# Router products by column groups of TensorE, the second attention's state over normalised tokens, and new orders in both passes

## The chip, the cores and the metric

One Trainium2 chip, one core of it. The metric is the device time of one execution in microseconds. The kernel before was timed three times. The core has TensorE (PE: matmuls; PEld: its weight loads), VectorE (DVE), ScalarE (ACT), GpSimd (POOL) and the engine that issues most DMAs (SP). Each works through a program of its own in order, and they meet in semaphores.

## The reference, cut to what matters

Two layers over 8 x 1024 tokens of 256 features, each an attention and a mixture of 8 experts. The change touches the router of both mixtures and the second attention:

```
# router, both layers:  logits = tokens @ gate.T          (256 features -> 8 experts)
#                       top1 = argmax, rank by cumsum, keep while rank < capacity
# second attention, per batch of 1024 tokens, x = layernorm(tokens):
qkv = einsum('bnd,ed->bne', x, W_qkv);  q, k, v = split(qkv, 3)
q = relu(q) + 1e-6;  k = relu(k) + 1e-6
kv = einsum('bnd,bne->bde', k, v)
z = 1 / (einsum('bnd,bd->bn', q, k.sum(axis=1)) + 1e-6)
out = einsum('bnd,bde,bn->bne', q, kv, z) @ W_out.T + b_out
x = x_in + layernorm(out)
```

## The kernel before, in words

The 8192 tokens are 16 groups of 512 (four tiles of 128); two groups, a pair, are one batch. Products that need full precision are made of three fp32r matmuls (high x high, high x low, low x high: `three`), so each operand is kept as a high part (ACT, a copy that rounds) and a low part (DVE, value minus high part).

The program has these stages: a memory part; pass 1 (loop `for s in range(1, 14)`: first attention, gate, feed-forward and router of layer 1, a group per step, each step working on groups s-2 to s+3); the 8 experts of layer 1; pass 2 (loop over pairs: second attention and router of layer 2); the 16 expert halves of layer 2. Expert tokens are scattered to DRAM by POOL's indirect DMAs and read back by SP.

The order in each engine is written out by hand, as one loop per engine with the calls of several groups interleaved. Nothing reorders it. PE's results go through a ring of three PSUM units (`Ring`, two banks each; `unit` takes the next one and waits until the reader of its last content has freed it) beside one accumulator, `acc`. So the call that comes three units later waits for the ACT or DVE instruction that empties a unit.

The router (`logits`, L707 to L714): for each of four tiles and two halves of the features one fp32 matmul with the tile's 128 x 128 tokens as weights and 8 columns of the gate's weights moving; it gives tokens on partitions, and DVE (`route1`) takes the argmax. `route1` leads to the one-hot rows, PE's `prefix` to the ranks, `route2` to the slots, POOL's `scatter` to DRAM.

The second attention. ACT normalises a group into `xnA` (`xl_norm`), PE turns it (`xl_t`), ACT and DVE split it (`xl_high`, `lows`). PE then makes `queries` (12 matmuls of 512 columns), `keys` (24 of 512 columns: K and the values V, already folded with W_out, side by side) and `state` (24 of 256 or 258 columns: K transposed times V, with a column of ones for the sum of the keys). DVE applies relu and 1e-6 (`q_relu`, `k_relu`), ACT copies V (`v_copy`) and rounds (`kv_high`, `q_high`), DVE subtracts (`kv_low`, `q_low`). At a batch's end ACT and DVE split the accumulated state (`kw_high`, `kw_low`), and a pair later PE makes `att_out` (24 of 258 columns per group). `unread` is matmuls whose result nobody reads; they stand where PE would be idle.

## Time and profile before

| | us |
|---|---|
| median of 3 runs | 1897.04 |
| lowest, highest | 1894.91, 1899.98 |
| profiled execution, its span from first to last instruction | 1900.1 |
| PE, PEld busy in it | 1843.4, 1631.5 |
| DVE, ACT, POOL busy | 1496.8, 1069.6, 624.2 |
| pass 2 (1180 to 1477) | 297 |

The profiled execution has only its span; what lies around the first and the last instruction is not in the trace. Busy times are unions of the instructions' durations. A matmul's duration contains its latency, and following matmuls overlap it, so that what one costs PE is read as the distance from start to start.

### The profile page before, as it was taken

The page shows a single profiled execution, that of the slowest core. Times are in us where ns is not written, and L with a number is a line of the kernel's source. Part 1 is how long each engine was busy: PE and PEld are TensorE (multiplying, and loading weights), DVE is VectorE, ACT ScalarE, POOL GpSimd, SP SyncE. Part 2 cuts the span into 40 slices and gives each one's busy share as a digit, 9 for nine tenths or more (in the row PEclk, how much of TensorE's full clock was granted, in tenths as well). Part 3 has the DMA queues.
Part 4 walks back from the last instruction along what each step waited for, and adds up shares of the span by engine and source line. Part 5 has one row for each costly group of instructions (what it writes and reads, how often), then busy time and mean ns, then how long its engine had stood idle before and what let it go on. Part 6 is the DMA issues. An engine that isn't in the chain of part 4 may idle for free.

```text
span 1900.1 us, 31592 instructions
## 1 busy us (share of the span) xinstructions
PE 1843.4 (97%) x11542; PEld 1631.5 (86%) x11542; DVE 1496.8 (79%) x3901; ACT 1069.6 (56%) x1734; POOL 624.2 (33%) x927
## 2 busy tenths in 40 slices
PE   8999999999999999999899999999999999999996
PEld 7888878888888888888779998888988799999996
DVE  7777579999999999999748884789998566666663
ACT  5656725566566665666456663665564255555552
POOL 3211001234433333444604443134534312333333
PEclk9999999999999999999899999999999899999998
DMA  5545242222222221201143422134322312222210
GB/s 178 163 150 167 81 153 68 90 86 95 89 84 83 94 82 64 78 26 37 51 152 124 134 87 89 60 119 135 100 89 76 90 60 82 93 83 86 76 51 18
DMA packets 132610, 176.95 MB, mean 93 GB/s; under 512 B 11486, under 2 KB 115813, under 8 KB 132328
## 3 DMA queue, kind: packets, MB, share of 16 engines
q1 hardware_dynamic: 121704, 159.87, 26.3%
q0 software_dynamic: 10752, 15.06, 2.3%
q8 instruction: 92, 1.51, 0.3%
q14 instruction: 62, 0.51, 0.1%
HBM read 113.25 MB, written 76.51 MB: 100 GB/s over the span
## 4 chain that ended last, share of the span: by engine, by line
PE 86%; DVE 5%; ACT 2%; POOL 2%; DMA 2%; issue 2%; SPq 0%; POOLq 0%; DVEq 0%; ACTq 0%
PE ps L385 78%; PE ps L409 4%; PE ps L712 2%; PE ps L701 1%; POOL d_p L2587 1%; DVE bst L1614 1%; PE ps L470 1%; DMA stage<-in_w 0%; DMA stage<-in_wi 0%; DVE rO L2155 0%; DMA xa<-in_x 0%; DVE wslotA L1820 0%; DMA d_x<-df 0%; DVE pay L1939 0%; DVE kl L1639 0%
## 5 line engine op out<-in xcount | busy, mean ns | idle before, releaser
L385 PE MATMUL ps<-wslotA,fh 128*128 128x256 f32 x1776 | 326.1, 284 | 0.0
L1830 DVE TENSOR_TENSOR fl<-fF,fh 128x512 fp32r<-128x512 f32 x316 | 214.0, 683 | 94.2 <-ACT fF L1209 93.3
L385 PEld LDWEIGHTS ps<-wslotA,fh 128*128 128x128 f32 x1776 | 280.4, 191 | 5.2 <-DVE fl L1830 0.2
L385 PE MATMUL ps<-wslotA,fl 128*128 128x256 f32 x888 | 251.2, 283 | 0.0
L2582 POOL TENSOR_TENSOR smalls<-smalls,powers 128x4 f32<-128x4 f32 x87 | 28.0, 321 | 591.7 <-DVE smalls L1617 591.6
L2587 POOL DMA_INDIRECT d_p<-pay,sut x128 | 154.3, 1205 | 103.7 <-DVE pay L1987 57.4
L385 PE MATMUL ps<-x2h,wslotA 128*128 128x512 f32 x512 | 171.0, 396 | 0.2 <-DVE x2l L1639 0.2
L385 PEld LDWEIGHTS ps<-wslotA,fl 128*128 128x128 f32 x888 | 170.0, 191 | 0.0
L1208 ACT ACTIVATE fh<-ps,b1e 128x512 fp32r<-128x512 f32 x126 | 86.9, 690 | 143.0 <-PE ps L385 140.6
L385 PE MATMUL ps<-wslotB,fh 128*128 128x256 f32 x752 | 137.1, 283 | 0.4 <-DVE fl L1830 0.4
L385 PE MATMUL ps<-eh,wslotB 128*128 128x512 f32 x384 | 125.3, 393 | 2.4 <-DVE el L2011 2.4
L385 PE MATMUL ps<-eh,wslotA 128*128 128x512 f32 x384 | 125.5, 393 | 0.7 <-DVE el L1639 0.7
L385 PEld LDWEIGHTS ps<-wslotB,fh 128*128 128x128 f32 x752 | 119.2, 192 | 3.1 <-issue 0.6
L1208 ACT ACTIVATE fh<-ps,cols 128x512 fp32r<-128x512 f32 x128 | 88.6, 692 | 56.6 <-PE ps L385 52.8
L385 PEld LDWEIGHTS ps<-x2h,wslotA 128*128 128x128 f32 x512 | 96.3, 188 | 24.7 <-issue 5.6
L385 PE MATMUL ps<-wslotB,fl 128*128 128x256 f32 x376 | 106.4, 283 | 0.0
L385 PE MATMUL ps<-x2l,wslotA 128*128 128x512 f32 x256 | 100.2, 391 | 0.0
L2587 POOL DMA_INDIRECT out_x<-eq,sut x60 | 69.5, 1159 | 91.1 <-DVE eq L2052 76.9
L2583 POOL TENSOR_TENSOR smalls<-smalls,powers 128x4 f32<-128x4 f32 x87 | 95.4, 1096 | 6.8
L1628 DVE SCALAR_TENSOR_TENSOR xl<-xl,smalls,rows 128x256 f32<-128x256 f32 x192 | 80.0, 479 | 15.6 <-POOL smalls L2583 15.6
L1614 DVE BATCH_NORM_STATS2 bst<-xl 128x6 f32<-128x256 f32 x256 | 89.4, 411 | 0.3
L1209 ACT ACTIVATE fF<-ps,cols 128x512 f32<-128x512 f32 x128 | 88.3, 690 | 0.0
(383 smaller groups left out, 5146.5 us busy)
## 6 DMA issues: line engine op xcount, KB each, us to landing
stage<-in_w SPq DMA_DIRECT2D x16, 1024.0 KB, 5.6
d_p<-blank SPq DMA_DIRECT2D x24, 528.0 KB, 4.8
pay<-d_p SPq DMA_DIRECT2D x24, 528.0 KB, 3.7
d_x<-df SPq DMA_DIRECT2D x16, 516.0 KB, 3.5
xA<-d_x SPq DMA_DIRECT2D x16, 516.0 KB, 3.7
xa<-in_x SPq DMA_DIRECT2D x16, 512.0 KB, 4.9
d_h<-hh SPq DMA_DIRECT2D x16, 512.0 KB, 5.4
d_h<-hl SPq DMA_DIRECT2D x16, 512.0 KB, 3.0
```

The source lines that it names most:

```text
L385: return pe.matmul(o, a, b, start=start, stop=stop, skip_group_check=True)
L409: t = pe.transpose(ps[:, c * 512 + i * 128:c * 512 + i * 128 + 128], x[:, i * stride + c * 128:i * stride + (c + 1) * 128], ident)
L470: t = pe.transpose(ps[:, i * 256 + c * 128:i * 256 + c * 128 + 128], x[:, c * 512 + i * 128:c * 512 + i * 128 + 128], ident)
L712: t = pe.matmul(ps[:, i * 8:i * 8 + 8], x[:, c * 512 + i * 128:c * 512 + i * 128 + 128], w8[:, c, :], start=c == 0, stop=c == 1)
L1208: act.activation(dh[:, half(k)], u.ap[:, half(k)], func, bias=b)
L1209: t = act.activation(df_[:, half(k)], u.ap[:, half(k)], func, bias=b)
L1614: marks.append(mark(ve.bn_stats(b[:, i, :], x[:, i, :])))
L1628: marks = [mark(ve.scalar_tensor_tensor(x[:, i, :], x[:, i, :], m[:, i:i + 1], gain, ALU.subtract, ALU.mult)) for i in range(4)]
L1830: ve.tensor_tensor(dl[:, half(k)], df_[:, half(k)], f32(dh[:, half(k)]), ALU.subtract).then_inc(S["low"], 1)
L2582: last(po.tensor_tensor(t[:, 8:12], mv_of(t)[:, :, 1], eps, ALU.add))
L2583: po.tensor_tensor(t[:, 12:16], t[:, 8:12], mhalf, ALU.pow).then_inc(signal, 1)
L2587: po.indirect_dma_start(dst, bass.IndirectOffsetOnAxis(idx[:, i:i + 1], 0), src[:, i, :], None, bounds_check=bound, oob_is_err=False).then ...
```

## The change

Four things. First, the router's product turns round: the gate's 8 columns are the weights, 128 tokens move, and the four tiles' results go to PSUM partitions 0, 32, 64 and 96, which are four groups of 32 columns of PE's array. ACT then copies the 128 x 128 block to `lgt` (`logits_copy`) and PE turns it back in one transpose (`by_token`), so that `route1` reads tokens on partitions as before.

Second, the state is summed over the normalised tokens U instead of over the values: K transposed times U (256 columns), and once per batch that state times the folded value weights (`state_values`, 12 matmuls of 258 columns). So `keys` makes only K (24 matmuls of 256 columns), and V is never formed. `state_high`, `state_low` split the state, `u_high`, `u_low` the tokens.

Third, since a normalised token's features sum to zero, its last feature is replaced by 1 and the last row of the weights is subtracted from the others (`weights_differences`, once, on DVE in the last expert of layer 1). The column of ones gives the sum of the keys, and 1e-6 sits in a weight row, so that relu(k) + 1e-6 is one maximum: ACT applies Relu as it reads PSUM (`q_high`, `k_high`), DVE takes max and subtracts in one instruction (`q_low`, `k_low`). `q_relu`, `k_relu` and `v_copy` go.

Fourth, the loops of all engines in pass 2 are written anew, the router's calls in pass 1 are moved, the second expert weight block of layer 2 is loaded three pairs later and split in the loop's step 6 instead of step 2, and `unread` calls at the end of pass 2 go, except the last of 52.

PE in pass 1, one step, before, then changed (xl is a group's tokens, x1h and x1l the gate's operand, x2h the feed-forward's, sc the attention's weights, tT the turned tokens):

```order
L385 MATMUL ps<-small,x1h 128x256 x2
L385 MATMUL ps<-small,x1l 128x256
L712 MATMUL ps<-gwT,tT 128x8 x8
L385 MATMUL ps<-xl_93,sc_97 128x258 x2
L385 MATMUL ps<-halo,sc_97 16x258
```

```order
L390 MATMUL ps<-x2l,wslotA 128x512
L390 MATMUL ps<-x2h,wslotA 128x512
L390 MATMUL ps<-tT,gwT 8x128 x8
L390 MATMUL ps<-small,hh_70 128x512 x2
L390 MATMUL ps<-small,hl_72 128x512
```

The eight products have moved ahead of the gate's matmuls; the transpose (L723) stands some 50 rows later, behind the first `w2`:

```order
L390 MATMUL ps<-wslotA,fh_111 128x256 x2
L390 MATMUL ps<-wslotA,fl_113 128x256
L723 MATMUL ps<-ident,lgt 128x128
L390 MATMUL ps<-x2h,wslotA 128x512
L390 MATMUL ps<-x2l,wslotA 128x512
```

DVE in pass 2, a stretch that begins at a group's statistics in a pair's step. Before (kvF is relu(K) beside V, kvl its low part, qF relu(Q), ql its low part, rO the attention's output, pay the tokens for the router, cdt and lgx router rows):

```order
L2135 TENSOR_TENSOR kvl_132<-kvF_130,kvh_134 128x1024
L2126 TENSOR_SCALAR kvF_131<-ps 128x2x256
L1939 TENSOR_TENSOR pay_55<-rO_136,xb_138 128x4x256
L2166 SCALAR_TENSOR_TENSOR smalls<-smalls 128x4
L1614 BN_STATS bst<-pay_55 128x6 x4
L1617 BN_AGGR pay_55<-bst 128x2 x4
L2119 TENSOR_SCALAR qF<-ps 128x1024
L2135 TENSOR_TENSOR kvl_133<-kvF_131,kvh_135 128x1024
L2131 TENSOR_TENSOR ql_144<-qF,qh_141 128x1024
L2126 TENSOR_SCALAR kvF_130<-ps 128x2x256
```

Changed (kk_l is K's low part, ul the tokens', xAl the turned tokens'):

```order
L1997 TENSOR_TENSOR pay_56<-rO_136,xb_138 128x4x256
L2178 SCALAR_TENSOR_TENSOR ql_145<-ps,qh_142 128x1024
L2183 SCALAR_TENSOR_TENSOR kk_l<-ps,kk_h 128x512
L2188 TENSOR_TENSOR ul_133<-xnA,uh_131 128x1024
L2235 SCALAR_TENSOR_TENSOR smalls<-smalls 128x4
L2183 SCALAR_TENSOR_TENSOR kk_l<-ps,kk_h 128x512
L1672 BN_STATS bst<-pay_56 128x6 x4
L1675 BN_AGGR pay_56<-bst 128x2 x4
L1697 TENSOR_TENSOR xAl_127<-ps,xAh_125 128x512 x2
```

Two instructions per half group (kvF from PSUM, kvl over 1024 columns) have become one over 512 columns that reads PSUM, and that one now comes behind ACT's Relu, no longer ahead of ACT.

ACT in pass 2, where tokens are rounded, changed:

```order
L1101 ACTIVATE lgt<-ps 128x128
L1101 ACTIVATE uh_131<-xnA 128x1024
```

The first of the two empties the router's unit; the second waits for the state of the group before last (`u_high` below), and everything of ACT's step behind it waits with it.

The diff, cut to its core:

```diff
             def logits(which, g, x, w8):
-                ps = unit("LG", which, g)
-                for i in range(4):
-                    for c in range(2):
-                        t = pe.matmul(ps[:, i * 8:i * 8 + 8], x[:, c * 512 + i * 128:c * 512 + i * 128 + 128], w8[:, c, :],
-                                      start=c == 0, stop=c == 1)
-                t.then_inc(S["lg"], 1)
+                ps = unit("LA", which, g)
+                for c in range(2):
+                    for i in range(4):
+                        t = mm(ps[32 * i:32 * i + 8, 0:128], w8[:, c, :], x[:, c * 512 + i * 128:c * 512 + i * 128 + 128],
+                               c == 0, c == 1)
+                t.then_inc(S["la"], 1)
+            def by_token(which, g):
+                evacuated("LA", which, g)
+                pe.transpose(unit("LG", which, g)[:, 0:128], lgt, ident).then_inc(S["lg"], 1)
...
             def keys(g, k):
-                    t = three(ps[:, half(i % 2)], [(xAh[g % 2][:, q[c]], xAl[g % 2][:, q[c]], wq_h[:, c, 256:768],
-                                                    wq_l[:, c, 256:768]) for c in range(2)], True, True)
+                    t = three(ps[:, i % 2 * 256:i % 2 * 256 + 256],
+                              [(xAh[g % 2][:, q[c]], xAl[g % 2][:, q[c]], wq_h[:, c, 256:512], wq_l[:, c, 256:512])
+                               for c in range(2)], i % 2 == 0, True)
...
             def state(g, k):
-                        mm(o, hv[:, i, q], hv[:, i, 256:514], first, False)
-                        mm(o[:, 0:256], hv[:, i, q], lv[:, i, 256:512], False, False)
-                        t = mm(o, lv[:, i, q], hv[:, i, 256:514], False, end)
+                        t = three(acc[:, half(c, 256)], [(uh[g % 2][:, q], ul[g % 2][:, q], hv[:, i, :], lv[:, i, :])],
+                                  first, end)
+            def state_values(bt):
+                pe.wait_ge(S["stl"], bt + 1)
+                ps = unit("KW", bt)
+                for m in range(2):
+                    q = slice(m * 128, m * 128 + 128)
+                    t = three(ps[:, half(m, 258)], [(st_h_[:, c, q], st_l_[:, c, q], wx_h[:, c, :], wx_l[:, c, :])
+                                                    for c in range(2)], True, True)
...
+            def logits_copy(which, g):
+                copy(lgt, u.ap[:, 0:128]).then_inc(u.free, 1)
+            def u_high(g):
+                if g >= 2:
+                    act.wait_ge(S["sta"], 2 * (g - 1))
+                act.wait_ge(S["xn_l"], 2 * g + 1)
+                copy(uh[g % 2], xnA).then_inc(S["xn_l"], 1)
             def q_high(g):
-                act.wait_ge(u.free, u.before + 1)
-                copy(qh[g % 3], qF).then_inc(S["qh"], 1)
+                act.wait_ge(S["q"], g + 1)
+                act.activation(qh[g % 3], ring.of("Q", g).ap, ACT.Relu).then_inc(S["qh"], 1)
-            def v_copy(g, k):
-            def kv_high(g, k):
+            def k_high(g, k):
+                act.activation(kk_h[:, half(k)], ring.of("K", g, k).ap[:, 0:512], ACT.Relu).then_inc(S["ksh"], 1)
...
-            def q_relu(g):
-            def k_relu(g, k):
             def q_low(g):
-                ve.tensor_tensor(ql[g % 3], qF, f32(qh[g % 3]), ALU.subtract).then_inc(S["ql"], 1)
+                ve.scalar_tensor_tensor(ql[g % 3], u.ap, 1e-6, f32(qh[g % 3]), ALU.max, ALU.subtract).then_inc(u.free, 1)
+            def k_low(g, k):
+                ve.scalar_tensor_tensor(kk_l[:, half(k)], u.ap[:, 0:512], 1e-6, f32(kk_h[:, half(k)]), ALU.max,
+                                        ALU.subtract).then_inc(u.free, 1)
+            def u_low(g):
+                ve.tensor_tensor(ul[g % 2], xnA, f32(uh[g % 2]), ALU.subtract).then_inc(S["ul"], 1)
+            def weights_differences():
+                last(ve.tensor_tensor(wqk_v, wqk_v, wlast.unsqueeze(1).to_broadcast([128, 2, 512]), ALU.subtract))
...
@@ PE, pass 2 @@
                 if s in PAIRS:
                     queries(2 * s)
+                if s - 1 in PAIRS:
+                    state_values(s - 1)
+                if s in PAIRS:
+                    keys(2 * s, 0)
+                    keys(2 * s, 1)
...
@@ SP @@
-                if s in (0, 1):
-                    weights(19 + s)
+                if s in (0, 4):
+                    weights(19 + s // 4)
```

## Rows read from the trace of the kernel before

**Rows 1.** The page: the span, the engines' busy time, the chain that ended last.
```profile
span 1900.1 us, 31592 instructions
PE 1843.4 (97%) x11542; PEld 1631.5 (86%) x11542; DVE 1496.8 (79%) x3901; ACT 1069.6 (56%) x1734; POOL 624.2 (33%) x927
...
PE 86%; DVE 5%; ACT 2%; POOL 2%; DMA 2%; issue 2%; SPq 0%; POOLq 0%; DVEq 0%; ACTq 0%
```

**Rows 2.** Busy time by stretch; granted clock, DMA share and GB/s last.
```profile
290.00:915.00 625.00, 624.61 (x4088) 550.90 (x4087) 576.93 (x1578) 388.79 (x610) 220.13 (x376) 1.00 0.22 72
...
1180.00:1477.00 297.00, 286.52 (x1871) 256.77 (x1872) 255.11 (x728) 164.68 (x268) 115.78 (x180) 0.98 0.31 95
```

**Rows 3.** The same view, single steps: pass 2, then pass 1.
```profile
1226.31:1262.34 36.03, 31.44 (x188) 28.17 (x187) 30.19 (x74) 23.25 (x36) 11.41 (x20) 0.91 0.42 129
1262.34:1298.13 35.79, 35.79 (x244) 32.15 (x244) 31.82 (x98) 20.96 (x35) 15.68 (x26) 1.00 0.39 115
1298.13:1333.98 35.85, 35.85 (x244) 32.19 (x244) 33.02 (x100) 20.97 (x35) 15.80 (x26) 1.00 0.39 116
410.92:453.55 42.63, 42.63 (x282) 37.42 (x282) 39.62 (x112) 26.84 (x43) 14.88 (x27) 1.00 0.30 101
```

**Rows 4.** PE in order of time, pass 1: start, duration, instruction, count.
```profile
451.85 1.85 PE L712 MATMUL ps<-gwT,tT 128*128 128x8 f32 x16
453.55 3.70 PE L385 MATMUL ps<-xl,sc 128*128 128x258 f32 x14
457.18 0.50 PE L385 MATMUL ps<-x2h,wslotA 128*128 128x512 f32 x1
```

**Rows 5.** PE in order of time, 239 to 242 us.
```profile
239.13 2.08 PE L385 MATMUL ps<-xT 128*128 128x144 f32 x16
241.04 0.52 PE L385 MATMUL ps<-xT,xT 128*128 128x16 f32 x4
241.49 0.60 PE L385 MATMUL ps<-ident,cols 128*1 128x128 f32 x4
242.02 0.33 PE L547 MATMUL ps<-ident,gs 128*128 128x128 f32 x1
```

**Rows 6.** PE in order of time, pass 2.
```profile
1308.87 0.40 PE L385 MATMUL ps<-small,xAl 128*128 128x512 f32 x1
1309.11 0.28 PE L385 MATMUL ps<-kvh 128*128 128x258 f32 x1
...
1310.55 0.40 PE L385 MATMUL ps<-xAh,small 128*128 128x512 f32 x1
...
1313.35 1.04 PE L701 MATMUL ps<-ident,pay 128*128 128x128 f32 x8
```

**Rows 7.** DVE by line and shape, three pairs (1262.34 to 1369.73).
```profile
L2135 DVE TENSOR_TENSOR kvl<-kvF,kvh 128x1024 fp32r<-128x1024 f32 x12 | 14.6, 1215 | 0.0
L2126 DVE TENSOR_SCALAR kvF<-ps 128x512 f32<-128x512 f32 x12 | 8.2, 687 | 3.3 <-PE ps L385 3.1
L1639 DVE TENSOR_TENSOR xAl<-ps,xAh 128x512 fp32r<-128x512 f32 x12 | 7.6, 675 | 0.0
L2119 DVE TENSOR_SCALAR qF<-ps 128x1024 f32<-128x1024 f32 x6 | 7.3, 1225 | 2.7 <-PE ps L385 2.7
L2145 DVE TENSOR_TENSOR small<-ps,small 128x516 fp32r<-128x516 f32 x3 | 2.0, 663 | 0.0
```

**Rows 8.** ACT by line and shape, the same three pairs.
```profile
L1071 ACT ACTIVATE kvh<-kvF 128x1024 fp32r<-128x1024 f32 x12 | 12.8, 1069 | 0.3
L1075 ACT ACTIVATE xnA<-xA,smalls 128x256 f32<-128x256 f32 x24 | 12.4, 588 | 0.0
L1071 ACT ACTIVATE kvF<-ps 128x512 f32<-128x512 f32 x12 | 7.1, 593 | 24.1 <-DVE kvF L2126 24.1
L1279 ACT ACTIVATE lgx<-lgx 128x32 f32<-128x32 f32 x6 | 1.4, 228 | 0.0
```

**Rows 9.** The chain that ended last, in order of time, 1241 to 1256 us.
```profile
1241.92 8.66 DMA stage<-in_w
...
1250.61 1.07 ACT wslotA L1071
...
1255.64 5.50 PE ps L385 x24
```

**Rows 10.** PE in order of time, the end of pass 2 and the first expert.
```profile
1465.77 0.50 PE L385 MATMUL ps<-small,qh 128*128 128x258 f32 x2 [1.89 <-DVE small L2145]
...
1474.03 1.85 PE L712 MATMUL ps<-wgT,tTO 128*128 128x8 f32 x16
...
1511.20 0.50 PE L385 MATMUL ps<-eh,wslotA 128*128 128x512 f32 x1 [0.73 <-DVE el L1639]
```

More of the change, by code:

```diff
@@ L265, in build @@
         xAl = [tile("xAl0", 4, R), tile("xAl1", 8, R)]
-        qF = tile("qF", 6)
-        kvF = [tile("kvF0", 7), tile("kvF1", 18)]
-        kvl = [tile("kvl0", 9, R), tile("kvl1", 10, R)]
-        kvh = [at(f"kvh{i}", TILES_AT + 11 * PAGE + i * 4 * 1032, 1028, R) for i in range(2)]
+        kk_h, kk_l = tile("kk_h", 6, R), tile("kk_l", 7, R)
+        uh = [tile("uh0", 9, R), tile("uh1", 11, R)]
+        ul = [tile("ul0", 10, R), tile("ul1", 12, R)]
+        stt = tile("stt", 13, R)
+        st_h_, st_l_ = v3(stt[:, 0:512], 2, 256), v3(stt[:, 512:1024], 2, 256)
+        wqk_v, wlast = v3(stage[:, 0:1024], 2, 512), stage[:, 1024:1536]
         wv_v = v3(stage[:, 1536:2048], 2, 256)
@@ L950, in tensor_program @@
             logits(0, 15, tT, gwT)
+            unread(a12_h, 2)
+            by_token(0, 15)
             unread(a12_h, 4)
@@ L1020, in tensor_program @@
                     state(2 * s + 1, 1)
-                if s + 1 in PAIRS:
-                    xl_t(2 * s + 3)
+                if s - 1 in PAIRS:
+                    by_token(1, 2 * s - 2)
+            state_values(7)
+            t_t(1, 13)
             prefix(1, 12)
@@ L1329, in values_folded @@
             def values_folded():
                 act.wait_ge(S["vw"], 1)
-                copy(wq_h[:, :, 512:768], two(ring.of("VW").ap)).then_inc(S["vwh"], 1)
+                copy(wx_h[:, 0, 256:258], blank[:, 0:2])
+                copy(wx_h[:, 1, 256:258], ident[:, 127:128].to_broadcast([128, 2]))
+                copy(wx_h[:, :, 0:256], two(ring.of("VW").ap)).then_inc(S["vwh"], 1)
                 act.wait_ge(S["w1"], 8 * (G + E))
-                for k in range(2):
-                    for i in range(2):
-                        copy(v3(kvh[k], 2, 514)[:, i, 512:514], ones[:, 0:2])
+                for i in range(4):
+                    copy(xv(xnA)[:, i, 255:256], ones[:, 0:1])
@@ L1337, in kw_high, with state_high @@
+            def state_high(bt):
+                if bt:
+                    act.wait_ge(S["vw"], bt + 1)
+                act.wait_ge(S["sta"], 4 * (bt + 1))
+                copy(st_h_, v3(acc, 2, 512)[:, :, 0:256]).then_inc(S["kwh"], 1)
             def kw_high(bt):
@@ L2111, in expert_end, with x_low, q_low @@
                     o.then_inc(S["eres"] if h else S["eres_h"], 1)
[L2114 removed]
+            def x_low(g):
+                lows(xAl[g % 2], xAh[g % 2], ring.of("XLT", g), S["xlh"], g)
+            def q_low(g):
                 u = ring.of("Q", g)
[L2116 to L2127 removed]
@@ L2508, in vector_program @@
                     new_x(1, 2 * s - 1)
+                if s in PAIRS:
+                    state_low(s)
+                if s - 1 in PAIRS:
                     route1(1, 2 * s - 2)
+                if s + 1 in PAIRS:
+                    q_low(2 * s + 2)
+                if s - 1 in PAIRS:
                     stats_5th(1, 2 * s - 1)
@@ L2513, in vector_program @@
                 if s + 1 in PAIRS:
-                    lows(xAl[(2 * s + 3) % 2], xAh[(2 * s + 3) % 2], ring.of("XLT", 2 * s + 3), S["xlh"], 2 * s + 3)
+                    k_low(2 * s + 2, 0)
+                    k_low(2 * s + 2, 1)
+                    u_low(2 * s + 3)
+                if s - 1 in PAIRS:
+                    route2(1, 2 * s - 2)
+                if s in PAIRS:
+                    att_out(2 * s, 0)
+                    att_out(2 * s, 1)
+                if s + 1 in PAIRS:
+                    x_low(2 * s + 3)
+                if s in PAIRS:
+                    stats_o(2 * s)
+                    att_out(2 * s + 1, 0)
+                    att_out(2 * s + 1, 1)
+                    nmean_o(2 * s)
+                    stats_o(2 * s + 1)
+                if s - 1 in PAIRS:
+                    route1(1, 2 * s - 1)
+                if s in PAIRS:
+                    new_x(1, 2 * s)
+                if s + 1 in PAIRS:
+                    q_low(2 * s + 3)
+                    k_low(2 * s + 3, 0)
+                if s == 2:
+                    weights_low(19, 0)
+                    weights_low(19, 1)
+                if s == 6:
+                    weights_low(20, 0)
+                    weights_low(20, 1)
             for n in range(E - 1, 3 * E):
@@ L2956, in sync_program @@
             weights(4)
-            load(b1e[:, :], io["eb1_c"], S["b1e"])
+            load(b1e[:, :], io["eb1_c"], S["late"])
             square(wout_v, "WoutT", S["wout"])
```

363 lines of the change are left out of this document (177 added, 186 removed), and 2 rows, old and new, of the table S.

## The prediction

> **What bounds the kernel now.** I read the page first. PE is busy for 1843.4 of 1900.1 us and holds 86% of the chain that ended last [rows 1], so a change pays by what it takes off PE, as long as no other engine steps in. Then the stages: in the main part of pass 1 PE is busy for 624.6 of 625 us at full clock, in pass 2 for 286.5 of 297 [rows 2]. Then single steps: a pair of groups in pass 2 takes 35.8 us, a step of pass 1 about 42.6, with PE busy throughout and DVE busy for 32 to 33 and 39.6 of it [rows 3]. DVE is at 91% and 93%: it is the next bound, and close. Last the distances between PE's starts: twelve matmuls of 512 columns in 1313.35 - 1310.55 = 2.80 us, 0.233 each; twelve of 256 or 258 in 1310.55 - 1309.11 = 1.44, 0.12 each [rows 6].
>
> **Pass 2 on PE, per pair.** `keys` stays at 48 matmuls, of 256 columns instead of 512: 48 x (0.233 - 0.12) = 5.4 us less. `state` keeps its 48 of about 256 columns. `state_values` adds 12 x 0.12 = 1.4. Queries, `att_out` and transposes are unchanged. With the router (next part, 0.25 less per group) the pair comes to 35.8 - 5.4 + 1.4 - 0.5 = 31.3 us.
>
> **The router's products.** Before, a group has 16 records (two per fp32 matmul) in 453.55 - 451.85 = 1.70 us [rows 4]. Afterwards there are 16 again, with 8 weight columns and 128 moving. The nearest row is a product with one weight column and 128 moving ones: four records in 242.02 - 241.49 = 0.53, 0.13 each [rows 5]. To this comes a change of the weights' width. Sixteen fp32 records of 144 columns take 1.91 us [rows 5], 0.83 ns per column, so fourteen of 258 should take 3.0; where widths of 128 and 16 columns alternate they take 457.18 - 453.55 = 3.63 [rows 4] with four changes of width, 0.16 us per change. The new block has two changes, 0.3 us. The transpose back adds about 0.13 (eight took 0.87 or so between neighbours).
>
> If the four column groups really run side by side, the block is four records deep: 4 x 0.13 + 0.3 + 0.13 = 1.0 us, 0.7 less than now. If nothing overlaps, it is 16 x 0.107 to 0.13, plus 0.43: 2.1 to 2.5, that is 0.4 to 0.8 more. No row shows two column groups at once. I take the middle: PE takes matmuls in order and the two records of one product follow each other in the same group, so a product can overlap its neighbour but not itself, which leaves eight of 0.13, 1.0 + 0.43 = 1.45 us, 0.25 less per group. In pass 1, which is PE's alone, that is 16 x 0.25 = 4 us.
>
> The rows show 0.16 us lost at each change of width [rows 4]. The Trainium skill says in TensorEngine Tiling (Array Packing), Tiling Modes, that a change of tiling mode drains the engine; by that rule the 0.3 us stays even where the products overlap in full, and the trace agrees in size.
>
> **Pass 2 on DVE, per pair.** Out go 4 `kvl`, 4 `kvF` and 2 `qF`: (14.6 + 8.2 + 7.3) / 3 = 10.0 us [rows 7]. In come 4 `k_low` over 512 columns out of PSUM, like xAl at 0.68: 2.7; 2 `u_low` over 1024, like kvl, 1.2 each: 2.4; one `state_low`, like the split state, 0.66 [rows 7]: 5.8 together. 32.4 - 10.0 + 5.8 = 28.2 us busy. Before, DVE's 32.4 busy went with a step of 35.8, 90.5%, the rest being gaps between dependent small instructions and waits of a few tenths. At the same share 28.2 gives 31.2 us: DVE reaches PE's 31.3. Neither alone sets the pair any more, and two orders that just touch don't mesh without loss: `q_low` and `k_low` now come behind ACT's Relu (1.07 for 1024 columns, 0.59 for 512 [rows 8]) where DVE used to read PSUM first. The PSUM unit is thus held for ACT plus DVE (about 1.3 us for K, 2.3 for Q), and three units later PE wants it. I take 31.7 per pair; bounds 30.5 (PE with the router overlapped in full) and 34. Eight pairs: 8 x (35.8 - 31.7) = 33 us less.
>
> ACT: out go 4 `kvh` (4.3 us) and 4 `kvF` copies (2.4); in come 4 K roundings (2.4), 2 `u_high` (2.1), `state_high` (0.6) and two copies of 128 columns (between the 0.23 of 32 columns and 0.59 [rows 8], 0.6 together). 21 busy becomes 20 of 31.7 [rows 3, 8]: it does not bound by its sum, only by its place (rival E).
>
> **The second weight block.** In the step 1226 to 1262 PE is busy for 31.4 of 36.0 us, at clock 0.91 [rows 3]: the block's load lands at 1250.6, ACT and DVE then split it, and PE starts again at 1255.6 [rows 9]. The load now comes three pairs earlier than its split, so this 4.6 us wait goes. What is late next in that step is DVE with 30.2 busy, so I count 3 less (0 to 5).
>
> **What gets longer.** At the last batch's end PE now waits for split state, product and split product instead of one split. Before, one split kept PE waiting for 1.89 us [rows 10]; the second one (0.6 ACT, 0.66 DVE) and the product (1.44) are partly covered by a transpose and `prefix`: +2. In the other batches `queries` (2.8 us) covers the first split, and two K blocks with a transpose (3.7) the second; if DVE runs late, this is where it shows. `weights_differences` puts a 1024-column subtraction (1.2) and smaller ones on DVE ahead of `low(2, 0)` in the last expert of layer 1: +1. From the last `att_out` (1474.0) to the first expert of layer 2 (1511.2) there are 37 us [rows 10] that DVE, ACT, POOL and DMAs set; the `unread` calls removed there only filled PE's idle time. The router's extra step costs one ACT copy and one transpose (0.5 us with hand-over) and gives back what PE's block loses: 0. The same at the end of pass 1. In pass 1 the transpose comes only after the first `w2`, and `route1` some 6 us later than before; `prefix` is 20 us away and the feed-forward's low parts have about 4 us in hand before PE asks for them, so nothing is late.
>
> **The sum** against the profiled execution: 1900.1 - 33 - 3 - 4 + 2 + 1 = 1863. The timed median lies 3.1 us below that span (1897.0 against 1900.1), so I predict 1860 us.
>
> **The rivals.**
> A. The forecast: 1860, own range 1850 to 1870. Chance 0.5.
> B. The column groups overlap in full: 0.45 us less per group than in A, 7 us in pass 1; in pass 2 PE's pair is 30.4 and DVE sets it at 31.2, another 4 or 5. For it: consecutive products go to different groups. Against: the two records of one product do not. Time 1848. Chance 0.2. The Trainium skill, TensorE: Matmul & The Clock Gate, Part 3 (Packing small matmuls), gives 4 ns per further tile and a measured 2.38 times for three column tiles: by its model this is the case, while its in-order rule is what A rests on. No run here shows either yet.
> C. They don't overlap, and PE only gets two changes of width and a transpose: 2.1 to 2.5 us per block. Against A that is 0.65 to 1.05 x 16 = 10 to 17 us; in pass 2 half of it is hidden behind DVE, so 8 to 13 in all for pass 1 and 4 to 8 more. 1881. Chance 0.13.
> D. DVE takes over in pass 2: the products gain as in A, but gaps bring the pair to 34 us, 8 x 2.3 = 18 more: 1878. For it: 28.2 busy within 31.7 leaves as little as before, with more hand-overs per step. Against: DVE's share before was the same and cost PE 0.0 idle in two steps [rows 3]. Chance 0.1.
> E. Slower than before: the single buffer `xnA`. A group's tokens are normalised (4 x 0.59 [rows 8]), turned, rounded by `u_high`, subtracted by `u_low`, and only then may the next be normalised; `u_high` also waits for the state of the group before last, and ACT's queue stands behind it: the output's normalisation, Q's and K's Relu, hence PSUM units, hence PE. I find ACT free some 3 us before that state ends in each pair's middle. If each group's block of 3.2 us reached PE, 16 x 3.2 = 51 more: 1911. It decides from (1897 - 1860) / 16 = 2.3 us lost per group. Against: DVE has work queued in that time, and only one of a pair's two groups is placed so tightly. Chance 0.07.
>
> **From these the range.** B's and C's ends give 1842 to 1882; outside lie E and a slice of C and D. Less than 0.3% (5.7 us) is no change that a measurement of this kernel can tell. A to D are faster by more, 0.93 less a little for a mixture of C, D and E that just cancels: 0.91 faster, 0.03 the same, 0.06 slower.
>
> **What the changed profile would show.** The router's 16 records start over about 1.3 us (A), 0.8 (B) or 1.7 to 2.1 (C), and a pass 1 step is 42.3, 41.9 or 43 us. A pair in pass 2 takes about 31.7 with PE above 97% busy; at 34 or more with waits of PE on DVE low parts it is D, with waits on `xnA` and ACT idle before `uh` it is E. No idle of 4.6 us before a `base` or `kvl` instruction. Wrong would be the whole sum if the pair stayed above 34, or if the 37 us between passes grew with PE's clock down for want of the `unread` calls.

## The result and the profile after

| | kernel before | changed kernel | ratio, 95% interval |
|---|---|---|---|
| median | 1897.63 us (1894.91 to 1899.98, 4 runs) | 1887.68 us (1886.32 to 1889.31, 4 runs) | 0.9948 [0.9936, 0.9960] |
| span of the profiled execution | 1900.1 us | 1884.6 us | |

The change makes the kernel 0.5% faster. Forecast were 1860 us and a range of 1842 to 1882: the sign was right, the size was not. The medians differ by 10.0 us and the profiled spans by 15.5. Where both are known, the timed value lies 1.7 us above the span (1886.32 and 1884.6 for the profile of the changed kernel); the profiled execution of the kernel before was thus a slow one (about 1901.8, an estimate, above all four timed ones), and that of the changed kernel the fastest of its four. Of the balance below, 5.5 us are this. First the page of the changed kernel: the head, busy times by engine, and the chain that ended last.

```profile
span 1884.6 us, 31885 instructions
PE 1787.1 (95%) x11647; PEld 1576.6 (84%) x11647; DVE 1467.6 (78%) x3884; ACT 1067.6 (57%) x1760; POOL 632.8 (34%) x927
PE 70%; DVE 14%; POOL 6%; issue 5%; ACT 3%; DMA 2%; SPq 0%; another core or an unknown queue 0%; POOLq 0%; DVEq 0%; ACTq 0%
```

PE has lost 56 us of busy time (1843.4 before [rows 1]), but the span fell by 15.5 only, and PE's share of the chain fell from 86% to 70%. DVE and POOL took it. Where, the busy times by stretch say (columns: stretch, length, then busy us of PE, PEld, DVE, ACT and POOL with counts, granted clock, DMA share, GB/s): pass 1, one of its steps, pass 2, and the end of pass 2.

```profile
293.00:890.00 597.00, 575.79 (x3782) 498.74 (x3781) 536.95 (x1474) 360.33 (x566) 206.44 (x347) 0.98 0.22 72
524.00:568.50 44.50, 41.56 (x280) 36.05 (x280) 40.81 (x114) 27.26 (x43) 17.45 (x31) 1.00 0.27 90
1200.00:1458.00 258.00, 240.52 (x1975) 221.40 (x1975) 218.47 (x690) 155.37 (x271) 118.42 (x179) 1.00 0.35 110
1458.00:1505.00 47.00, 33.43 (x186) 26.68 (x186) 25.23 (x98) 14.46 (x27) 17.32 (x22) 0.75 0.29 90
```

In pass 1, where PE was busy for 624.6 of 625 us [rows 2], it now idles 21 of 597. A step took 42.6 us [rows 3]; it now takes 44.5 (43.9 and 45.1 by turns; the first two, at 41.4 and 42.6, are not yet held up). The starts of PE's landmarks give the balance:

| PE's start of | before | after | difference between landmarks |
|---|---|---|---|
| first matmul of the first expert (layer 1) | 968.91 | 987.25 | +18.3 |
| first `queries` of pass 2 | 1180.18 | 1201.14 | +2.6 |
| last `att_out` | 1473.91 | 1456.96 | -37.9 |
| first matmul of layer 2's experts | 1511.20 | 1495.68 | +1.4 |
| end of the span | 1900.1 | 1884.6 | 0.0 |

Pass 2 gave more than forecast, and half of it was lost in pass 1. What PE waits for in pass 1, between 293 and 890 us (columns: in total, times, longest):

```profile
PE ps L414 <- DVE x2l L1697: 17.6, 10, 1.9
PE ps L414 <- DVE xl L1691: 3.6, 1, 3.6
```

Once a step, PE waits for DVE's `x2l`: the matmuls at L414 are `x1_t`, which transpose the next group's `xl` into the PSUM unit that `x2l` has just left. The chain of waits in one step, in order of time (start, us, what):

```profile
437.22 22.54 PE ps L390 x132
459.76 0.12 PE ps L723
...
459.98 0.20 DVE lgx L2014
...
461.32 0.19 DVE oht L2025
461.52 1.15 DVE xl L1946
...
462.69 1.41 DVE bst L1672 x4
464.10 0.29 DVE smalls L1675 x4
...
464.45 0.56 POOL smalls L2652
...
467.64 1.12 POOL d_p L2657
...
469.06 3.28 POOL d_p L2657
...
472.64 0.98 POOL d_p L2657
...
473.93 1.05 POOL smalls L2653
...
475.00 1.67 DVE xl L1686 x4
476.68 1.58 DVE xl L1691 x4
478.26 1.21 DVE x2l L1697 x2
...
479.61 1.22 PE ps L414 x8
```

It starts at the transpose back (L723, `by_token`), which stands 22.5 us into PE's step. Behind it come `route1` (L2014 to L2025), the sum with the attention (L1946) and the second norm's statistics on DVE, one root on POOL, then the scatter's four indirect DMAs, which POOL's order puts ahead of the root of the first norm (L2653 at 473.93). For this root DVE waits, and `x2l` and PE behind it. PE's next step starts with it, so that the chain closes on itself: a step can't be shorter than the chain. The kernel before had the same scatter on POOL ahead of the same root; there `x1_t` found `x2l` done:

```profile
473.52 1.67 DVE L1628 SCALAR_TENSOR_TENSOR xl<-xl,smalls,rows 128x256 f32<-128x256 f32 x4 [1.19 <-POOL smalls L2583]
475.11 1.67 DVE L1633 SCALAR_TENSOR_TENSOR xl<-xl,smalls,rows 128x256 f32<-128x256 f32 x4
476.70 1.28 DVE L1639 TENSOR_TENSOR x2l<-ps,x2h 128x512 fp32r<-128x512 f32 x2
```

That is DVE before: `x2l` ended at 477.98, and `x1_t` started at 479.42, 1.4 us later. This was all the slack that this way had, and `route1` had started 1.3 us behind the router's product, not 17. DVE had been waiting for POOL already.

The router's block itself, on PE of the changed kernel in pass 1 (start, us of one, line, operation, tiles, count): what stands ahead of the sixteen records, the records, what follows, and the transpose back with its neighbours.

```profile
487.15 0.39 PE L390 MATMUL ps<-x2l,wslotA 128*128 128x512 f32 x1
487.37 0.39 PE L390 MATMUL ps<-x2h,wslotA 128*128 128x512 f32 x1
487.69 0.62 PE L390 MATMUL ps<-tT,gwT 128*8 128x128 f32 x16
488.25 0.73 PE L390 MATMUL ps<-small,hh 128*128 128x512 f32 x2
...
548.44 0.28 PE L390 MATMUL ps<-wslotA,fl 128*128 128x256 f32 x1
548.56 0.27 PE L723 MATMUL ps<-ident,lgt 128*128 128x128 f32 x1
548.59 0.48 PE L390 MATMUL ps<-x2h,wslotA 128*128 128x512 f32 x1
```

From 487.69 to 488.25 is 0.56 us for what took 1.70 [rows 4], and the transpose costs 0.12 or less. The change of width ahead of the block comes on top: from the last product of 512 columns to the block are 0.32 us, where such a product elsewhere takes 0.23. Together that is 0.77 us: per group PE has 0.93 us less to do in the router, not 0.25.

### The profile page after: what moved, and what is told of

Read it like the earlier page. It is cut to its first block, busy times and chain, and to the rows that moved or that the text cites. A ratio compares the mean times of both kernels' runs of the same rounds, so it can differ in the third digit from the quotient of the medians.

```text
span 1884.6 us, 31885 instructions
## 1 busy us (share of the span) xinstructions
PE 1787.1 (95%) x11647; PEld 1576.6 (84%) x11647; DVE 1467.6 (78%) x3884; ACT 1067.6 (57%) x1760; POOL 632.8 (34%) x927
## 4 chain that ended last, share of the span: by engine, by line
PE 70%; DVE 14%; POOL 6%; issue 5%; ACT 3%; DMA 2%; SPq 0%; another core or an unknown queue 0%; POOLq 0%; DVEq 0%; ACTq 0%
PE ps L390 65%; POOL d_p L2657 4%; PE ps L414 3%; DVE bst L1672 2%; DVE xl L1686 1%; DVE xl L1691 1%; POOL smalls L2653 1%; DVE xl L1946 1%; PE ps L706 1%; DVE x2l L1697 1%; PE ps L475 1%; DVE pay L1997 1%; DVE rO L2224 1%; POOL smalls L2652 1%; DMA qc<-in_Wg1T 0%
## 5 line engine op out<-in xcount | busy, mean ns | idle before, releaser
L2657 POOL DMA_INDIRECT d_p<-pay,sut x128 | 158.1, 1235 | 76.3 <-issue 38.3
L390 PE MATMUL ps<-x2h,wslotA 128*128 128x512 f32 x512 | 177.1, 409 | 0.0
L2653 POOL TENSOR_TENSOR smalls<-smalls,powers 128x4 f32<-128x4 f32 x87 | 94.7, 1088 | 6.8
```

What stands on the lines that cost most here:

```text
L390: return pe.matmul(o, a, b, start=start, stop=stop, skip_group_check=True)
L2653: po.tensor_tensor(t[:, 12:16], t[:, 8:12], mhalf, ALU.pow).then_inc(signal, 1)
L2657: po.indirect_dma_start(dst, bass.IndirectOffsetOnAxis(idx[:, i:i + 1], 0), src[:, i, :], None, bounds_check=bound, oob_is_err=False).then ...
```

## The experiments

Twelve runs were made, in three jobs of four, each job on one chip. Theory A: the chain above holds pass 1. Theory B: DVE is full in pass 1. (The recorded text of run 1 uses the same letters for a coarser question: whether the loss sits in the router's new order at all.)

**1. Pass 1's router and orders as before, pass 2 as changed.** PE, ACT and DVE of pass 1 go back to the old product by tokens, without `logits_copy` and `by_token`.

> The changed kernel with pass 1's router as before: products with tokens as weights, no copy and no turn back, and pass 1's PE, ACT and DVE orders as before; pass 2 as changed. Theory A (the whole loss sits in pass 1's new order of the router, +18 us up to the experts; pass 2's 38 us gain stands alone): a pass 1 step back from 44.5 to 42.6 us, total 1887.7 - 18 = 1870, within 3. Theory B (the loss is in what pass 1 inherits from elsewhere, its weights or memory layout): the step stays at 44.5, total near 1887.

Measured: 1864.92 us (1861.92 to 1866.28), ratio to before 0.9822 [0.9805, 0.9838]. The step is 42.55 us again and PE waits for `x2l` once, 0.2 us. So the loss sits in pass 1, and pass 2 alone is worth some 34 us. The time is 5 us below the 1870 expected; the way from the first `queries` to the last `att_out` is 3.4 us shorter here than in the first job, in the same code (252.4 against 255.8; runs 9 and 10 take this up), and the first expert starts 19.8 us sooner, not 18.

**2. The transpose back earlier.** PE as below; DVE in pass 1 in the order of before.

```
                 if s - 2 in GROUPS:
+                    by_token(0, s - 2)
+                if s + 2 in GROUPS:
                     attend(s + 2, 0)
                     attend(s + 2, 1)
                 if s in GROUPS:
                     ff_in(s, 2, 0)
                     w2(s, 0)
-                if s - 2 in GROUPS:
-                    by_token(0, s - 2)
```

> The changed kernel, with the transpose back (by_token) ahead of attend on PE and DVE's order in pass 1 as before (route1 right behind difference). Theory A (a chain closes on itself in each step: by_token on PE, route1, combined and stats on DVE, POOL's root behind the scatter, affine_1st and x2l on DVE, PE's x1_t; route1's wait for by_token puts 0.7 us of idle and 1.5 us of work into it): the chain is cut, PE bounds again at 42.6 - 1.0 = 41.6 us per step, 13 steps x 2.9 = 38 less, 1850, within 6. Theory B (DVE's sum bounds the step, 40.8 busy of 44.5 with gaps): no change, 1888.

Measured: 1859.53 us (1855.17 to 1862.62), 0.9790 [0.9770, 0.9811]; a step 42.4 us. It helps, less than expected: PE still waits for `x2l`, 5.7 us in nine waits. The chain no longer goes through the transpose. It starts at PE's last gate product, for which DVE waits (L1929, which reads it; the kernel before waited 0.25 us there), and has `route1` within it:

```profile
491.81 0.69 DVE L1929 TENSOR_TENSOR gt<-ps,rows 128x512 f32<-128x512 f32 x1 [0.71 <-PE ps L390]
```

From the end of the gate's products (the transpose's start at 491.61) to `x1_t` are 26.9 us. In the kernel before the same way took PE 27.6 us (451.85 to 479.42), of which 1.70 were the router's product; with 0.12 for the transpose instead, PE would need 26.0 (an estimate). So here it is the router's gain itself, 1.6 us on this way, that uses up the 1.4 us of slack. Moving the transpose alone is not enough.

**3. `route1` late.** DVE only; PE keeps the transpose where the change put it.

```
                 if s - 1 in GROUPS:
                     new_x(0, s - 1)
-                if s - 2 in GROUPS:
-                    route1(0, s - 2)
                 if s + 1 in GROUPS:
                     combined(s + 1)
                     stats_2nd(s + 1)
+                if s - 2 in GROUPS:
+                    route1(0, s - 2)
```

> The changed kernel, DVE only: in pass 1 route1 stands behind stats_2nd instead of ahead of combined. PE as changed. Theory A: 0.7 us of idle and 1.5 of work leave the chain ahead of POOL's root: 2.1 us less until stats_2nd ends, the step falls from 44.5 to about 42.4 if stats_1st were still behind route1, so 13 x 2 = 26 less: 1862, between 1850 and 1870. Theory B (DVE's sum): only the 0.7 idle per step goes, 1879.

Measured: 1850.21 us (1848.71 to 1850.96), 0.9746 [0.9730, 0.9762]; a step 41.64 us. Pass 1 by stretch, and its waits of PE (all that are listed):

```profile
293.00:880.00 587.00, 586.27 (x3933) 508.81 (x3931) 552.45 (x1514) 373.86 (x589) 211.07 (x354) 1.00 0.22 74
```

```profile
PE ps L414 <- DVE xl L1691: 0.5, 1, 0.5
PE ps L390 <- DVE x2l L1697: 0.2, 1, 0.2
```

Seven small instructions moved behind the statistics, and the waits are gone: a better result than the 1862 expected, since the step falls to PE's own 41.64 us and not to 42.4. DVE is busy for 94.1% of the stretch, more than the 89.9% of the changed kernel: theory B falls, a fuller DVE holds nobody up.

**4. The root first.** POOL only: the root of the first norm ahead of the scatter.

```
+                if s + 3 in GROUPS:
+                    root(sm(0, s + 3), (S["var1"], s + 3 + 1), S["rs1"])
                 if s - 2 in GROUPS:
                     scatter(0, s - 2)
-                if s + 3 in GROUPS:
-                    root(sm(0, s + 3), (S["var1"], s + 3 + 1), S["rs1"])
```

> The changed kernel, POOL only: in pass 1 the root for the first normalisation stands ahead of the scatter of 4 indirect DMAs, not behind it. Theory A: the chain loses the scatter's 8 us on POOL, DVE's idle of 1.9 us ahead of affine_1st and PE's of 1.9 us ahead of x1_t go, the step falls to PE's 41.6: 1850, within 6. Theory B (DVE's sum is the bound; POOL's wait only takes idle that DVE has anyway): under 5 us less, 1884.

Measured: 1852.11 us (1851.60 to 1855.53), 0.9762 [0.9746, 0.9779]; a step 41.64 us. Cutting the chain in another place, on another engine, gives the same step: theory A is shown. Run 1 has the same pass 2 and PE full in pass 1 too, so the steps give what the router's new form is worth there: 42.55 - 41.64 = 0.91 us per group, beside 0.93 by the rows. Up to the first expert run 3 is 11.5 us ahead of run 1; of the 14.7 us between the two times the other 3 lie behind the last `att_out`, in code that is the same.

**5. Both remedies together.**

> Both remedies for pass 1 together: VectorE does route1 behind stats_2nd (as in the run with the late route1), and GpSimd does the root of the first norm ahead of the scatter (as in the run with the root first). Theory A (one chain from the router's transpose over VectorE and GpSimd to x1_t holds a step of pass 1, and either remedy opens it in full): PE is already the bound of a pass-1 step at 41.64 us with either, so both together give the same step, 41.6 us, and 1850 us. Rival: with one remedy something is still waited for that the other takes away (PE busy was 585.2 to 586.3 of 587 us in the stretch 293 to 880): then 1845 us or less, with a step under 41.5.

Measured: 1857.87 us (1854.63 to 1859.95), 0.9781 [0.9764, 0.9799]. A step is 41.64 us, as theory A has it, but the time is 7.7 us longer than run 3's. Nearly all of it is in pass 2 (7.1 us from the first queries to the last `att_out`): pairs of 32.1 instead of 30.7 us, in code that is the same. Runs 6 to 8, of the same job, show the same pairs; so pass 1's question is answered here by the step, and a new question is there (runs 9 to 11).

**6. Halves next to each other.** With `route1` late.

```
-                for c in range(2):
-                    for i in range(4):
+                for i in range(4):
+                    for c in range(2):
                         t = mm(ps[32 * i:32 * i + 8, 0:128], w8[:, c, :], ...
```

> The kernel with the late route1, and in the router's products the loops swapped: the two halves of one tile's sum stand next to each other, so that of 8 logical products two in a row go to the same column group. The changed kernel's 16 records, in which four in a row go to four different column groups, took 0.56 us from the first to the next product behind them. If the groups work side by side and records of one group stand in line, swapped products take longer: four groups with four records each one behind the other in the order of issue would be at most twice, 1.0 to 1.2 us a block, 31 to 32 blocks, +15 to +20 us on 1850 where PE is the bound: 1866. If the order of issue makes no difference (each group has a queue of its own), 0.56 us again and 1850. In between 0.6 to 0.9 us a block, 1852 to 1860.

Measured: 1858.20 us (1854.05 to 1860.03), 0.9783 [0.9763, 0.9802], beside 1857.9 of run 5. PE's rows:

```profile
523.75 0.64 PE L390 MATMUL ps<-tT,gwT 128*8 128x128 f32 x16
524.32 0.73 PE L390 MATMUL ps<-small,hh 128*128 128x512 f32 x2
```

0.57 us instead of 0.55 to 0.56, a step 41.67 instead of 41.64. The order within the block makes next to no difference: one product's records need not be kept apart. The single records' starts in the trace show how they run: four start within 0.02 us of each other (0.04 here), the next four 0.11 us behind the first four.

**7. The turned x first, at the start of pass 2.** ACT makes `xAh` of group 0 ahead of `uh`, DVE `xAl` ahead of `ul`.

> The kernel with the late route1, and at the start of pass 2 alone ScalarE copies the turned x (xAh of group 0) ahead of the copy of the tokens (uh), and VectorE makes xAl ahead of ul. The wait of the first queries for xAl was 2.4 us there (before the change 1.6). If the new copy and difference (uh 1.06, ul 1.23 us) stand in front of it, the wait falls by 1.1 to 2.2 us: 1848 us. If the wait is set by the normalised tokens themselves, nothing falls, 1850.

Measured: 1857.77 us (1854.66 to 1858.47), 0.9778 [0.9761, 0.9794]. PE's wait for `xAl` falls from 2.1 us (run 5) to 1.6, as in the kernel before. From the first expert to the first queries are 213.85 us, against 213.84 to 215.26 in runs 5, 6 and 8: half a microsecond, which the times can't show.

**8. Unread products back at the end of pass 2.** As below, and 4, 3 and 4 further down.

```
             by_token(1, 13)
+            unread(wq_h, 30)
             t_t(1, 14)
             prefix(1, 13)
+            unread(wq_h, 2)
             logits(1, 14, tTO, wgT)
...
```

> The kernel with the late route1, and at the end of pass 2 products that nobody reads stand again in PE's waits (30, 2, 4, 3 and 4 of 512 columns; before the change 12, 2, 4, 3 and 4). The granted clock in the stretch from the last att_out to the first expert product was 0.72 without them, and 0.86 in the kernel before. If the slower clock costs time there, the stretch of 37.3 us falls by about 1.5 us to that of before or less, and the time to 1848. If the end of pass 2 hangs on VectorE and GpSimd and not on PE, the clock rises and nothing is gained: 1850.

Measured: 1858.22 us (1854.50 to 1859.93), 0.9788 [0.9772, 0.9804]. The stretch from the last `att_out` to the first expert, here and in run 5 (one row each):

```profile
1426.00:1463.00 37.00, 30.07 (x170) 22.64 (x168) 19.43 (x86) 8.30 (x17) 17.23 (x23) 0.93 0.37 114
```

```profile
1430.00:1467.00 37.00, 23.19 (x129) 17.70 (x129) 19.52 (x86) 8.29 (x17) 17.47 (x23) 0.72 0.38 115
```

The granted clock rises from 0.72 to 0.93, and the stretch is 38.06 us against 38.15. PE is not its bound; the lower clock there costs no time that these two runs can show.

**9 and 10. `route1` late and the changed kernel again, on one chip.**

> The kernel with the late route1 once more, unchanged. In its first job its pairs of pass 2 took 30.7 us and it 1850.2 us; four variants of it in a second job took 32.1 us a pair and 1858 us, though their pass 2 is the same code at these pairs (and the kernel before took 1898.7 and 1898.9 in the two jobs). In the slow pairs ScalarE takes up the router's logits (lgt) 3.2 to 3.5 us after PE's last router product, once a pair, while GpSimd issues the scatter's indirect DMAs; in the fast ones 0.34 us after. Theory C (the chip or the job decides it): this run shows one or the other for all kernels of this job, and within the job it stands to the changed kernel by the whole loss of pass 1. Rival (the small edits of the second job did it): 1850 us and 30.7 us a pair whatever the chip.

> The changed kernel once more, beside the kernel with the late route1 on one chip. Its pairs took 31.9 us in the first run, with the late logits (3.1 to 3.2 us). Theory C: it shows the same kind of pair as the other runs of this job; with short pairs it takes about 1880, with long ones 1887. Theory A: the difference to the late route1 is pass 1 alone, 44.5 to 41.64 us a step and the end of the pass, 29 to 31 us.

Measured: 1850.44 us (1846.62 to 1853.11), 0.9744 [0.9726, 0.9762], and for the changed kernel 1879.78 us (1875.62 to 1881.06), 0.9892 [0.9876, 0.9909]. Both have pairs of 30.7 us. So the same kernel runs at 1887.7 in one job and 1879.8 in another, with the kernel before at 1897.6 to 1898.9 in all four jobs: theory C holds, the small edits of runs 5 to 8 did nothing to the pairs (whether it is the chip or the job can't be told, since each job had one chip). And on one chip the lost chain of pass 1 costs 1879.8 - 1850.4 = 29.3 us. What differs in the pairs shows on ACT. First the changed kernel of the first job: PE, then ACT (in brackets the idle time before, and who ended it), then POOL.

```profile
1393.65 0.62 PE L390 MATMUL ps<-tTO,wgT 128*8 128x128 f32 x16
1394.20 0.51 PE L390 MATMUL ps<-small,qh 128*128 128x258 f32 x2
```

```profile
1392.92 2.07 ACT L1105 ACTIVATE xnA<-xA,smalls 128x255 f32<-128x255 f32 x4
1397.52 0.28 ACT L1101 ACTIVATE lgt<-ps 128x128 f32<-128x128 f32 x1 [2.53 <-remote]
```

```profile
1393.09 0.98 POOL L2657 DMA_INDIRECT d_p<-pay,sut  x1 [0.31 <-issue]
1394.38 0.97 POOL L2657 DMA_INDIRECT d_p<-pay,sut  x1 [0.30 <-issue]
1395.65 0.97 POOL L2657 DMA_INDIRECT d_p<-pay,sut  x1 [0.30 <-issue]
```

And the same kernel in run 10, PE and ACT:

```profile
1392.12 0.62 PE L390 MATMUL ps<-tTO,wgT 128*8 128x128 f32 x16
1392.67 0.51 PE L390 MATMUL ps<-small,qh 128*128 128x258 f32 x2
```

```profile
1391.40 2.07 ACT L1105 ACTIVATE xnA<-xA,smalls 128x255 f32<-128x255 f32 x4
1393.36 0.26 ACT L1101 ACTIVATE lgt<-ps 128x128 f32<-128x128 f32 x1
```

PE goes on to its next product at 1394.20 in the one and at 1392.67 in the other; ACT takes the router's product up 3.3 us later in the one, 0.7 in the other, where it had been busy. It is not ACT alone that learns late. The trace has the time at which each semaphore was raised: in the first job that of the router's product at 1397.43, and only 0.13 us behind it the next of PE's, for an `att_out` whose last matmul had started at 1395.62; in run 10 the product's at 1392.79. So DVE's `smalls` (L2221), which waits for that `att_out`, comes 1.5 to 1.7 us later behind the product in a long pair (first job, run 5) than in a short one (runs 3 and 10). What is late is PE's signals, by up to 3 us. The product falls between POOL's indirect DMAs, but it does so in the short pairs too, at the same distances to a few hundredths of a us. In run 10:

```profile
1391.57 0.97 POOL L2657 DMA_INDIRECT d_p<-pay,sut  x1 [0.30 <-issue]
1392.84 0.98 POOL L2657 DMA_INDIRECT d_p<-pay,sut  x1 [0.31 <-issue]
```

The durations of the instructions are the same in both. PE's own starts don't slip at that place; they do so at three places later in the pair, two of them where PE waits for DVE's `ql` and `kk_l`, together by 1.2 to 1.4 us.

**11. Pass 2's router by tokens, as before.** With `route1` late; no column groups, no `lgt`, no transpose back in pass 2.

> The kernel with the late route1, and in pass 2 the router's product as before the change: by tokens, eight columns each, without the column groups, without ScalarE's copy lgt and without the transpose back. If the late signal of the router's product belongs to the column groups or to ScalarE's place in that chain, the pairs lose it: PE then has 1.70 instead of 0.56 us twice a pair (+2.0 to 2.3 us of PE work), so on a chip with short pairs 32 to 33 us a pair (1860 us), and on a chip with long ones the same or shorter than 32.1 (1857). If the late signal comes with any product there, a pair takes 33 to 34 us and the kernel 1866 us.

Measured: 1872.97 us (1871.41 to 1875.64), 0.9865 [0.9849, 0.9881], in the job with short pairs. A pair takes 34.5 us instead of 30.7. PE's busy time in a pair rises by 2.0 us (32.4 instead of 30.4), which is the router's work by the rows above, 2 x 0.93, or nearly. The rest is one wait, once a pair: the `queries` want the PSUM unit that holds the router's product, and DVE's `route1` (L2015) empties it late. PE by line, 1205 to 1420 us, the idle time ahead of it last:

```profile
L390 PE MATMUL ps<-xAh,small 128*128 128x512 f32 x102 | 36.1, 415 | 10.6 <-DVE lgx L2015 10.6
```

That is six waits of 1.8 us. In the changed form ACT's copy empties that unit. The time is 22.5 us above run 9's, more than either theory expected (1860 or 1866), and with the order fitted to this form some 10 of them might go; so the router's share of pass 2's gain lies between 12 and 22 us (an estimate). What this form does where pairs are long wasn't run.

**12. Sixteen records more, in one column group.** Ahead of each block of pass 1, nobody reads them.

```
+                if not which:
+                    for c in range(2):
+                        for i in range(4):
+                            mm(ps[0:8, 512 + i * 128:640 + i * 128], w8[:, c, :], ...
```

> The kernel with the late route1, and in pass 1 ahead of each router product in four column groups the same eight products (sixteen records) once more, all into one column group, the first, in the other bank of the unit; nobody reads them. Side by side in one kernel: if it is the groups that let products overlap, the sixteen records in one group take 1.2 to 1.8 us (before the change sixteen took 1.70) against 0.56 us in four groups. If it is the shape (128 columns of tokens past eight columns of weights) that is cheap, the block in one group takes 0.5 to 0.7 us too.

Measured: 1874.71 us, one run. A step goes from 41.64 to 43.36 us: sixteen records in one group, 0.11 us apart, cost 1.7 us, what they cost by tokens before the change, and 0.56 in four groups. It is the groups that let them overlap.

The times side by side. The pair is one of those past the middle of pass 2, where they are steady; the earlier ones take longer in every run (in run 3 up to 33.8 us).

| run | us | step of pass 1 | pair of pass 2 |
|---|---|---|---|
| kernel before | 1897.6 | 42.55 | 35.8 |
| changed kernel | 1887.7 | 44.5 | 31.9 |
| 10: changed, another job | 1879.8 | 44.5 | 30.7 |
| 1: router of pass 1 as before | 1864.9 | 42.55 | 30.7 |
| 2: transpose early | 1859.5 | 42.4 | 30.7 |
| 3 and 9: `route1` late | 1850.2, 1850.4 | 41.64 | 30.7 |
| 4: root first | 1852.1 | 41.64 | 30.7 |
| 5 to 8 | 1857.8 to 1858.2 | 41.64 to 41.67 | 32.1 |
| 11: router of pass 2 as before | 1873.0 | 41.64 | 34.5 |
| 12: sixteen records more | 1874.7 | 43.36 | 30.7 |

With one order of DVE put right the change is worth 2.5%, not 0.5%; the kernel of runs 3 and 9 is the best version found.

## Why the prediction was wrong

**The step that failed** is the last sentence on what gets longer: "In pass 1 the transpose comes only after the first `w2`, and `route1` some 6 us later than before; `prefix` is 20 us away and the feed-forward's low parts have about 4 us in hand before PE asks for them, so nothing is late." I followed `route1` to its readers, and `prefix` indeed never waits. But I did not ask what stands behind it in DVE's queue. `combined` and `stats_2nd` do, behind them POOL's root, the scatter and the next root, and behind these `x2l`. The slack on that way was 1.4 us, and the rows to see it by (DVE's 1.19 us of waiting on POOL, and PE's start 1.4 us behind `x2l`) were in the trace. Even with the transpose early, the 1.6 us that the router gives back on this way are more than the slack (run 2). Measured: +18.3 us up to the first expert instead of -4, an error of 22.3 us. The whole sum missed by 21.5 (1884.6 against 1863.1, not rounded): 22.3 here, 1.6 and 1.4 at the ends of pass 1 and 2, less 3.9 that pass 2 gave in addition. The forecast of the median missed by 27.7; the other 6.2 are the step from span to median. I took -3.1 over from the kernel before, whose profiled execution was a slow one; for the changed kernel it is +3.1. Runs 3 and 4 take the step's cause away from two sides, and the first expert then starts 13 and 10 us sooner than before the change.

**The router's block** was taken at 1.45 us with changes of width and transpose, from the argument that the two records of one product follow each other in one group. Measured 0.77: rival B's mechanism. Runs 6 and 12 show why: the time is set by the depth of a group, 4 records of some 0.11, whatever their order, and it was the argument on the order that failed. B's time of 1848 us is near what runs 3 and 9 reach, 1850, with one order of DVE changed. The Trainium skill's 2.38 times for three column tiles (TensorE: Matmul & The Clock Gate, Part 3) pointed the right way; here it was 1.70 / 0.56 = 3.0 for four. (In rival C the sum is muddled: 10 to 17 us for sixteen groups become 8 to 13 without a reason. Nothing in the result hangs on it.)

**The drain at a change of width**, two of 0.16 us in the forecast, is there and smaller: 0.09 us ahead of the block (0.32 instead of 0.23), and the product behind the block starts 0.20 us after the last record, where records stand 0.11 apart. That is 0.18 us in all. The Trainium skill says that a change of tiling mode drains TensorE (TensorEngine Tiling (Array Packing), Tiling Modes). The trace agrees; the size is from its rows alone.

**Pass 2** was forecast at -33 - 3 + 2 = -34 us, and came to -37.9 in the profiled execution (-42 in run 10). A steady pair was 31.9 against my 31.7, and that is luck, two errors that cancel: PE's work was less than I took it for (a pair takes 30.7 us where no signal is late, with PE busy for 30.4), and PE's late signals, which no row of before could show, gave 1.2 back. The earlier pairs, by the router's product at 31.4 to 34.7 us, I hadn't told apart. The 4.6 us wait ahead of the second weight block [rows 9] is gone as foreseen. DVE did not take over (D), and `xnA` held nobody up (E): PE's longest waits in the steady pairs are 0.5 us for `ql` and `kk_l`; over all of pass 2 the longest before its end is one of 1.5 for `lgt`, and one of 2.2 for `xAl` at its start.

**The ends.** `weights_differences` was counted +1; PE's waits there are 2.0 us for `el` and 2.2 for `xAl`, and the stretch grew by 2.6. The end of pass 2 was counted 0 and is 1.4 longer; in runs 3, 9 and 10 it takes 36.9 to 37.3 us, no more than before (37.3), so this goes with the job and not with the change. That the `unread` calls only filled idle time is right, as run 8 shows (0.93 instead of 0.72 of the clock, no time).

**Stays open:** why PE's signals come up to 3 us late once a pair in two of the four jobs, each on one chip, and not in the others. That POOL's indirect DMAs are the cause is not shown: they stand in the same place where nothing is late. What makes the earlier pairs of pass 2 longer wasn't looked into either.

## What to carry to other kernels

When an instruction moves to a later place in an engine's queue, follow not its readers alone but everything queued behind it, over every engine, until the way reaches the bound engine or closes on itself; what the move delays beyond the smallest slack on that way is the price, and what you take off the bound engine shortens the slack of every way beside it. A wait of 1 us on a side engine (here DVE on POOL) says that such a way is tight already, even where the bound engine never idles. And when a gain is missing, look for two places to cut the same chain: if both give the same step, the chain is shown.

## What the runs showed of the hardware

- Small fp32 products in four column groups overlap in full: sixteen records with 8 weight columns and 128 moving columns take 0.56 us in four groups (0.57 in the other order of the records) and 1.7 in one. Four records start nearly together, the next four 0.11 us later. Each change between this form and products over the full width cost 0.09 us; the one behind the block is within the 0.56.
- The third of the four indirect DMAs that POOL issues took 3.28 us where its neighbours took 1.0 to 1.1, and POOL's queue behind it stands for that time. In the kernel before it took 2.66 to 2.68. In run 3 no third one is long: in about half of the steps the four took 1.44, 0.97, 0.98 and 1.21, in the others the fourth took 3.27. What it depends on wasn't tried.
- The same program differed by 7.9 us between two jobs (1887.7 and 1879.8) where the kernel before differs by 1.3: in a tight mutual wait of PE, ACT and DVE, signals of PE that come up to 3 us late once a pair lengthen every steady pair by 1.2 to 1.4 us.
- A stretch of 38 us that other engines set took 38.15 us at a mean granted clock of 0.72 (run 5) and 38.06 at 0.93 (run 8).
